# Full tiles of a wide mixture-of-experts layer taken four at a time instead of two

## What is computed

```python
x = x + 0.5 * moe(layernorm(x))            # f0: E = 8 experts, K = 2 each token, inner width 176
scores = sigmoid(X @ gate_w.T);  idx = top_k(scores + router_bias, 2);  w = scores[idx] / sum
y_e  = (silu(X @ W1[e]) * (X @ W3[e])) @ W2[e]
out  = sum over the chosen e of w_e * y_e  +  a shared expert of inner width 352
```

## Time and profile before

| | us |
|---|---|
| median of 3 runs (lowest to highest) | 803.56 (803.04 to 803.93) |
| the profiled execution | 806.59 |
| its span, first to last instruction | 804.4 |
| TensorE busy | 712.2, 89% of the span |
| VectorE, ScalarE, GpSimd busy | 449.1, 407.7, 281.5 |
| `f0` full tiles, first time | 75.5 to 136.9 |
| `f0` full tiles, second time | 317.6 to 379.1 |

### The profile page before, as it was taken

How to read it: one execution, slowest core, us unless ns; L and a number is a source line. 1 busy time by engine, 2 the same in 40 slices (tenths; PEclk the granted TensorE clock), 3 DMA queues, 4 the chain that set the end, 5 groups by cost and what they waited for, 6 DMA issues and landing times.

```text
span 804.4 us, 14318 instructions
## 1 busy us (share of the span) xinstructions
PE 712.2 (89%) x4184; PEld 461.0 (57%) x4184; DVE 449.1 (56%) x1792; ACT 407.7 (51%) x974; POOL 281.5 (35%) x296
## 2 busy tenths in 40 slices
PE   5998999989898999999984889998899997689991
PEld 3446666464356446666452468656677775378651
DVE  5562333357646662333459664346898767844347
ACT  3831343327773841444327546533789777546530
POOL 0472244400000473244415756550011122646550
PEclk9999999999999999999995899998999999999996
DMA  8943344289999973344288265526000011255529
GB/s 295 316 167 113 108 140 124 89 266 351 351 351 350 352 262 119 96 140 130 89 265 348 104 194 159 149 98 209 1 2 1 2 42 41 92 187 158 152 96 313
DMA packets 102185, 137.18 MB, mean 171 GB/s; under 512 B 12224, under 2 KB 91136, under 8 KB 101504
## 3 DMA queue, kind: packets, MB, share of 16 engines
q1 hardware_dynamic: 88672, 98.52, 39.6%
q0 software_dynamic: 13440, 37.77, 12.9%
HBM read 57.41 MB, written 78.84 MB: 169 GB/s over the span
## 4 chain that ended last, share of the span: by engine, by line
PE 64%; DVE 12%; DMA 6%; ACT 6%; POOL 5%; issue 5%; SPq 1%; DVEq 0%; ACTq 0%; POOLq 0%
PE bank L1333 12%; PE bank L1112 11%; PE bank L1248 8%; POOL slot_rows L651 4%; PE bank L1269 4%; PE bank L1352 4%; PE bank L1425 3%; PE bank L1362 3%; DMA arena<-slot_rows 2%; PE bank L1500 2%; PE bank L1052 2%; DVE X L1679 2%; PE bank L1128 2%; DVE st L1697 2%; DVE X L1683 2%
## 5 line engine op out<-in xcount | busy, mean ns | idle before, releaser
L651 POOL DMA_INDIRECT f_result_rows<-arena x152 | 146.3, 963 | 184.0 <-ACT arena L811 165.1
L651 POOL DMA_INDIRECT slot_rows<-XN,slots x128 | 124.3, 971 | 227.5 <-DVE slots L1806 165.3
L1112 PE MATMUL bank<-XT,f_s 128*128 128x512 f32 (+1 forms) x256 | 120.4, 618 | 0.0
L1333 PE MATMUL bank<-w,arena 128*128 (+1 forms) x352 | 97.4, 479 | 0.0
L804 ACT ACTIVATE arena<-bank 128x128 f32<-128x128 f32 (+1 forms) x152 | 45.0, 296 | 98.4 <-PE bank L1333 57.6
L811 ACT ACTIVATE arena<-bank 128x256 f32<-128x256 f32 x152 | 54.5, 383 | 61.5 <-PE bank L1362 46.7
L1248 PE MATMUL bank<-w,arena 128*64 (+1 forms) x448 | 82.3, 387 | 0.2
L1112 PEld LDWEIGHTS bank<-XT,f_s 128*128 128x128 f32 (+1 forms) x256 | 47.3, 193 | 55.9 <-issue 55.6
L1333 PEld LDWEIGHTS bank<-w,arena 128*128 128x128 f32 (+1 forms) x352 | 50.3, 175 | 28.9 <-issue 9.6
L2087 DVE TENSOR_TENSOR arena<-arena,bank 128x176 f32<-128x176 f32 (+2 forms) x108 | 26.6, 274 | 67.0 <-ACT arena L804 67.0
L1248 PEld LDWEIGHTS bank<-w,arena 128*64 128x64 f32 (+1 forms) x448 | 53.5, 162 | 14.4 <-issue 1.7
(11 more groups left out here) (223 smaller groups left out, 1304.8 us busy)
## 6 DMA issues: line engine op xcount, KB each, us to landing
slot_rows<-zeros SPq DMA_DIRECT2D x16, 2312.0 KB, 20.3
arena<-slot_rows SPq DMA_DIRECT2D x104, 136.0 KB
XN<-f_result_rows SPq DMA_DIRECT2D x32, 256.0 KB, 5.3
Y<-f_result_rows SPq DMA_DIRECT2D x32, 256.0 KB, 6.2
arena<-slot_rows SPq DMA_DIRECT2D x96, 68.0 KB
w<-in_f_w SPq DMA_DIRECT2D x1, 4096.0 KB, 16.2
w<-in_f_w SPq DMA_DIRECT2D x1, 2816.0 KB
f_result_rows<-arena POOLq DMA_INDIRECT x152, 2.5
```

Of the source, the lines that this page charges most:

```text
L651: pool.indirect_dma_start(out=dst, out_offset=bass.IndirectOffsetOnAxis(ap=idx, axis=0), in_=src, in_offset=None).then_inc(done.sem, 16)
L1112: last = pe.matmul(bank[b + n % 2][0:kp, :], w[:, k, c * P:c * P + kp], XT[:, k, g * GW:(g + 1) * GW], start=(k == 0), stop=(k == KD - 1))
L1333: last = pe.matmul(of_tile(2, j, 2 * m.H)[lanes], p_xT[p % 2][:, 2 * i + k, lanes], L["w13"][:, k, e, :], start=(k == 0), stop=(k == KD - 1))
```

## The change

Full tiles of the wide layer go in fours, p = 0, 2, ... 12. TensorE does up(p), down(p-2), up(p+1), down(p-1), and then in one stretch on row halves turn(p+2), turn(p+3), rest(p-2), rest(p-1), hid(p), hid(p+1). The turned rows of two pairs lie side by side in banks 0 and 1, the inner columns of two pairs in banks 4 and 5, the results of two tiles in one bank (6 or 7). A reader of such a bank waits until both parts are written: ScalarE's copies of turned rows for both turns, VectorE's `turn_inner` for both hids, ScalarE's results for both rests. ScalarE's order in a four is four silus, four copies of turned rows, four results; VectorE's is the products of two pairs, four copies of inner columns, then `dest`. The pairs of split tiles keep their order. SyncE's and GpSimd's programs are unchanged. The diff without its asserts and unchanged branches:

```diff
+        def turned_half(r, p=0):
+            at = p % 2 * 2 * KD * HALF
+            return bank[r][:, at:at + 2 * KD * HALF].rearrange("p (c n) -> p c n", n=HALF)
+        def fours(m):
+            return range(0, m.FULL // 2, 2)
+        def with_next(m, p):
+            return p + 1 - p % 2 if p < m.FULL // 2 else p
+        def result_bank(p, i):
+            return bank[6 + i][:, p % 2 * D:(p % 2 + 1) * D]
+        def inner_half(r, p):
+            at = p % 2 * 3 * HALF
+            return bank[4 + r][:, at:at + 3 * HALF].rearrange("p (c n) -> p c n", n=HALF)
 
...
                 def y(j):
                     q, r = j % R, j // R
-                    act.wait_ge(*s["r_down"](j + 1))
+                    four = m.PAIRED and j // 2 < m.FULL // 2 - 2
+                    act.wait_ge(*s["r_down"](2 * (with_next(m, j // 2) + 1) if four else j + 1))
                     if j >= R:
                         act.wait_ge(*s["y_out"][q](16 * r))
-                    act.activation(ys[q], of_tile(6, j, D), ACT.Copy).then_inc(s["r_y"].sem, 1)
+                    act.activation(ys[q], result_bank(j // 2, j % 2) if m.PAIRED else of_tile(6, j, D), ACT.Copy
+                                   ).then_inc(s["r_y"].sem, 1)
 
...
                 def turn_pair(p):
-                    act.wait_ge(*s["r_xT_psum"](2 * (p + 1)))
+                    act.wait_ge(*s["r_xT_psum"](2 * ((p if p >= m.FULL // 2 + 2 else p + 1 - p % 2) + 1)))
                     if p >= 2:
                         act.wait_ge(*s["r_up"](2 * (p - 1)))
                     for r, rows in enumerate(HALVES):
-                        act.activation(p_xT[p % 2][:, :, rows], turned_half(r), ACT.Copy).then_inc(s["r_xT"].sem, 1)
+                        act.activation(p_xT[p % 2][:, :, rows], turned_half(r, p), ACT.Copy).then_inc(s["r_xT"].sem, 1)
 
...
+                def four(p):
+                    for j in range(2 * p, 2 * p + 4):
+                        silu(j)
+                    turn_pair(p + 2)
+                    turn_pair(p + 3)
+                    if p >= 2:
+                        for j in range(2 * p - 4, 2 * p):
+                            y(j)
...
                 def turn_pair(p):
                     for j in (2 * p, 2 * p + 1):
                         pe.wait_ge(*s["row_in"][j % R](16 * rows_due(m, j, j % R)))
-                    if p >= 1:
+                    if p % 2 == 0 or p >= m.FULL // 2 + 2:
                         pe.wait_ge(*s["r_xT"](2 * p))
                     for i in range(2):
                         for k in range(KD):
                             for r, rows in enumerate(HALVES):
-                                last = pe.transpose(turned_half(r)[:, 2 * i + k, :],
+                                last = pe.transpose(turned_half(r, p)[:, 2 * i + k, :],
                                                     xs[rows, (2 * p + i) % R, k * P:(k + 1) * P], ident[rows, rows])
                     last.then_inc(s["r_xT_psum"].sem, 2)
 
 
                 def hid_pair(p):
                     pe.wait_ge(*s["r_hid"](2 * (p + 1)))
-                    if p >= 1:
+                    if p % 2 == 0 or p >= m.FULL // 2:
                         pe.wait_ge(*s["r_hT"](2 * p))
                     for c in range(3):
                         for r, rows in enumerate(HALVES):
-                            last = pe.transpose(inner_half(r)[:, c, :], p_h[rows, p % 2, c * P:(c + 1) * P], ident[rows, rows])
+                            last = pe.transpose(inner_half(r, p)[:, c, :], p_h[rows, p % 2, c * P:(c + 1) * P], ident[rows, rows])
                     last.then_inc(s["r_hT_psum"].sem, 2)
 
                 def down_pair(p):
                     pe.wait_ge(*s["r_hT"](2 * (p + 1)))
-                    for j, c in ((2 * p, 0), (2 * p + 1, 2)):
-                        if p >= 1:
+                    if p < m.FULL // 2 - 2 and p % 2 == 0:
+                        pe.wait_ge(*s["r_y"](2 * p))
+                    for i, (j, c) in enumerate(((2 * p, 0), (2 * p + 1, 2))):
+                        if p >= m.FULL // 2 - 2:
                             pe.wait_ge(*s["r_y"](j - 1))
                         for lanes, e in whose(j):
-                            pe.matmul(of_tile(6, j, D)[lanes], p_hT[p % 2][:, c, lanes], L["w2"][0][:, e, :],
-                                      start=True, stop=False, skip_group_check=True)
+                            pe.matmul(result_bank(p, i)[lanes], p_hT[p % 2][:, c, lanes], L["w2"][0][:, e, :],
+                                      start=(p % 2 == 0 or p >= m.FULL // 2 - 2), stop=False, skip_group_check=True)
 
                 def rest_pair(p):
                     q = p % RESTS
                         part = slice(HALF * i, HALF * i + m.REST)
                         for n, (lanes, e) in enumerate(whose(j)):
                             w = p_rest[part, q, :] if n == 0 and (i or j >= m.FULL) else L["w2"][1][part, e, :]
-                            last = pe.matmul(of_tile(6, j, D)[lanes], p_hT[p % 2][part, 1, lanes], w,
+                            last = pe.matmul(result_bank(p, i)[lanes], p_hT[p % 2][part, 1, lanes], w,
                                              start=False, stop=True, skip_group_check=True)
                         last.then_inc(s["r_down"].sem, 1)
 
-                def pair(p):
-                    up_pair(p)
+                def next_experts(p):
                     for chunk in list_chunks(m):
                         if chunk[3] and chunk[3] == 2 * p + 4:
                             experts(*chunk)
+                def four(p):
+                    for n in (p, p + 1):
+                        up_pair(n)
+                        next_experts(n)
+                        if p >= 2:
+                            down_pair(n - 2)
+                    turn_pair(p + 2)
+                    turn_pair(p + 3)
                     if p >= 2:
-                        down_pair(p - 2)
                         rest_pair(p - 2)
+                        rest_pair(p - 1)
+                    hid_pair(p)
+                    hid_pair(p + 1)
+                def pair(p):
+                    up_pair(p)
+                    next_experts(p)
+                    down_pair(p - 2)
+                    rest_pair(p - 2)
                     if p + 2 < m.TILES // 2:
                         turn_pair(p + 2)
-                    if p >= 1:
+                    if p > m.FULL // 2:
                         hid_pair(p - 1)
...
                 if m.PAIRED:
                     turn_pair(0)
                     turn_pair(1)
-                    for p in range(m.TILES // 2):
+                    for p in fours(m):
+                        four(p)
+                    for p in range(m.FULL // 2, m.TILES // 2):
                         pair(p)
...
                 def turn_inner(p):
-                    dve.wait_ge(*s["r_hT_psum"](2 * (p + 1)))
+                    dve.wait_ge(*s["r_hT_psum"](2 * (with_next(m, p) + 1)))
                     if p >= 2:
                         dve.wait_ge(*s["r_down"](2 * (p - 1)))
                     for r, rows in enumerate(HALVES):
-                        dve.tensor_copy(p_hT[p % 2][:, :, rows], inner_half(r)).then_inc(s["r_hT"].sem, 1)
+                        dve.tensor_copy(p_hT[p % 2][:, :, rows], inner_half(r, p)).then_inc(s["r_hT"].sem, 1)
 
                 if m.PAIRED:
                     between = p_h[:, :, P:2 * P].rearrange("p b (i n) -> p b i n", i=2)[:, :, :, m.REST:HALF]
                     dve.memset(between, 0.0)
-                    for p in range(m.TILES // 2):
+                    for p in fours(m):
                         pair(p)
-                        if p >= 1:
+                        pair(p + 1)
+                        turn_inner(p)
+                        turn_inner(p + 1)
+                        dest(p // 2)
+                    for p in range(m.FULL // 2, m.TILES // 2):
+                        pair(p)
+                        if p > m.FULL // 2:
                             turn_inner(p - 1)
                         if p % 2 == 0:
                             dest(p // 2)
```

More of the change, by code:

```diff
@@ L79, in __init__ @@
         self.PAIRED = self.REST > 0
-        assert self.REST <= HALF and self.FULL % 2 == 0 and experts % 2 == 0
+        assert self.REST <= HALF and self.FULL % 4 == 0 and experts % 2 == 0
         self.KS = [min(P, shared - k) for k in range(0, shared, P)]
```

## The result

The changed kernel takes 828.45 us (median of 6 runs, 821.58 to 830.87), the kernel before 803.3 us (6 runs, 801.4 to 804.08). The ratio is 1.0316, 95% interval 1.0285 to 1.0348: slower by 3%. I had forecast slower, 820 with a range of 809 to 827, so the sign was right, the places of the loss too, and the size too small: the time lies 1.45 us above the range. The profiled execution took 829.79 us, span 827.6, against 806.59 and 804.4. Nearly all of the difference lies in the two loops of `f0`: from the first up to that of pair 17 they take 85.37 and 87.11 us (77.24 to 162.61, 331.17 to 418.28), before 74.97 and 75.09 (75.52 to 150.49, 317.62 to 392.71).

A forecast was written before the change was run, and what follows sets the result against it. TensorE was taken to bound the kernel, fed by SyncE's row loads. Switches -5.5, start +2.2, full fours +2.0, stalls +6.4 and +7.5, clock +4.0 sum to +16.6 us on 803.56: 820 us, range 809 to 827.

The forecast's parts named there:

- Switches, -5.5: TensorE's round trips into row halves: fourteen a layer become seven, 0.39 us each, saving 5.5 us over two layers.
- The place and the cause of the loss: SyncE's row loads wait on the later `dest`, leaving 2.15 us into a four, so TensorE waits for rows and rests.
- Full fours, 0.25 each, +2.0: Fours of full tiles: row loads and rests land without margin, 0.25 us lost in each of 8 fours, +2.0 us.
- The two stalls, 6.4 + 7.5: TensorE idles between the last four's turns, 3.2 us twice, and before pair 12's rest, 4.2 and 3.3 us.
- The clock, +4.0: After the stalls TensorE runs at half clock for 3.4 us, costing 2.0 us a layer, +4.0 us.
- The start, 2 x 1.1: Loop start: first up waits for both turns, +0.8 us; first four's hid and copies +0.3; two layers, +2.2 us.
- The one of a bound in every four, 825, at 0.20: Rival: scatter bursts make the dest-loads-turn-hid loop bind every full four, +4.7 us, and low clock lasts longer: 825 us, chance 0.20.
- The faster one: Rival: row loads and pair 12's rest arrive in time, leaving only switches and start, -3.3 us: 800.3 us, chance 0.08.

The follow-up runs named there:

- the first experiment: Changed kernel with `dest` moved back to right after the first pair's products of each four, on VectorE only: 801.49 us, ratio 0.9998.
- the second round: Changed kernel run again unaltered, beside the kernel before and three other edited kernels on one chip: 827.67 us, ratio 1.0303, against the kernel before.

## Why the prediction fell short

- **Switches, -5.5:** right. A full four of 8.59 us without waits, as worked out.
- **The place and the cause of the loss:** right. `dest` early again takes all of it away, `dest` late alone makes it. Loads left 2.14 us into a four (2.15), the second stall ended 152.78 - 145.46 = 7.3 into pair 14 and 406.77 - 399.38 = 7.4 in the second layer (7.8 and 6.9).
- **Full fours, 0.25 each, +2.0: this is the step that failed.** I had written that bursts of scatters come beside these loads, and then took the landing times of rows without such a burst. The five fours in the middle of a layer, from the second four's first up to the last four's, are 132.06 - 85.34 = 46.7 us in the first layer and 385.00 - 340.30 = 44.7 in the second against 5 x 8.59 = 43.0: 3.8 and 1.7 us of waits, 5.5 in both layers where I had 2.0. The kernel with only the last two `dest` early puts them at 6 to 7. I had also counted eight such fours where there are ten (p = 2 to 10 in two layers), which is 0.5 of it.
- **The two stalls, 6.4 + 7.5:** right in size; with the clock held 3.0 and 3.5 in the first layer, 3.6 and 3.5 in the second, against 3.2 in each and 4.2 and 3.3: 13.6 against 13.9.
- **The clock, +4.0: mis-sized.** I let it be low for 3.4 us and hid most of it under the second stall. In this profile it stayed low for 6.8 us, and the fall came while the first stall lasted, so the four's remaining rests and hids were slow before pair 14 could start (rests 0.63 instead of 0.38 each). Against the kernel that was kept busy there the clock costs 5.0 to 6.1 us, so 4.0 was too small by 1 to 2.
- **The start, 2 x 1.1:** 0.7 a layer for the wait on both turns is measured, and about 0.5 for the first four's own hid and copies can be read in the first experiment (from its first hid record to the next up 1.01 us instead of 0.46). That is 1.2 a layer. On top came, in the second layer, a low clock of 6.8 us where it had been 3.4; that was named as an end of the range, not put in the sum.
- **Rivals.** The one of a bound in every four, 825, at 0.20, was nearest to what happened: it held the late rows beside bursts and the longer stay at the low clock. None of the terms alone carries the miss; together they are the 3.5 of the fours, 1 to 2 of the clock and about 1 at the starts, against 23.2 - 16.6 = 6.6 in the profiles. The faster one needed a batch 3 us earlier in SyncE's queue; moving `dest` back gave that (the loads leave at 98.67, 4.3 us ahead of the four that wants them, instead of 2.1 into it), and 801.49.

## What to carry to other kernels

When work is gathered into longer stretches, everything that hangs behind the last of it moves as well: here four tiny VectorE instructions that give back load buffers. Follow each semaphore that a moved instruction raises to the queue that waits for it, add up that queue's issue times to the last transfer, and compare with when the data are first wanted; where the margin comes out near zero, take the slow landings, not the median, above all if the change also bunches other DMAs. A stall of some 3 us on TensorE costs its own length and more in the clock behind it: here four of them cost 13.6 us and another 5 to 6.

## What the runs showed that I had not expected

Unused matmuls made the kernel faster: eight records in each of four stalls, 819.82 against 827.67 us, of which 5 to 6 us can be laid to them. With scatters of 32 rows instead of 128 the second layer's full fours had no wait left (8.59 us instead of 8.94), though GpSimd issues as many of them: in this one execution it was the rows moved that slowed the neighbouring loads, not the number of instructions. And the times of the changed kernel lie 9.3 us apart (821.58 to 830.87) where those of the one before lay 2.7 apart in the same comparison. But in the second round the two spread alike, 822.24 to 831.87 and 797.05 to 806.06, so the change isn't shown to be the reason.
